# Decoder layer with linear attention on one core: a new order ahead of the first products and at the change of token halves, and output tiles in two banks

## The chip, the cores and the metric

One Trainium2 chip, one of its cores. The metric is device time in microseconds of one launch of the whole layer; the profile adds what each engine of the core did: TensorE (PE, with its weight loads as PEld), VectorE (DVE), ScalarE (ACT), GpSimd (POOL) and the queue of SyncE (SP), which issues transfers.

## What is computed

x is 2048 tokens (32 sequences of 64) by 512. Three steps, each with a residual:

```python
x = x + attn(layernorm(x))          # 32 heads of 128, decayed linear attention, gated
x = x + xattn(layernorm(x), ctx)    # cross attention, softmax over 512 positions
x = x + layernorm(x) @ identity.T
# attn: q, k, v = silu(h @ qkv_w.T); blocks of 32 tokens, scores decayed by head;
#       o * rsqrt(mean(o * o) + eps) * norm_w * sigmoid(h @ gate_w.T), then @ out_w.T
```

All in float32 precision. Only the first step is touched by the change.

## The kernel before

**Precision and products.** Each float32 operand is cut into a high part in a reduced format and a low part; a product is three matmuls (high by high, high by low, low by high). The projections use Strassen's scheme with seven block products in place of eight: the weights' blocks are mixed by four additions on GpSimd (mix, lines 302 to 309), the tokens' blocks by four subtractions (token_sums, lines 290 to 300). PRODUCTS (line 124) lists the seven with the bank that each adds to.

**Loops.** The tokens are two halves of 1024. For each half a body runs for d = 0 to 7 (quads of four heads): the first and the last body are written out, the six between are a hardware loop. A body is, on PE (lines 885 to 954): value products VA and VB (84 matmuls of 256 columns each), QK0, scores, QK1, scores, gate G01, weighing (two heads), QK2, output tiles 0 to 3 (rest_out), scores, QK3, output tiles 4 to 7, scores, G23, weighing. The second group's output tiles are made in the next body, in pairs behind VA, VB, QK0 and QK1. Each engine has its own list of the same body (GpSimd 337, ScalarE 505, VectorE 676), and only semaphores tie them. All orders are by hand.

**Within a call.** PE runs the seven products. The combinations go over snapshots: ScalarE copies a partial sum out of its bank (snapshot, line 431), VectorE adds it elsewhere (add_snapshot, 586), ScalarE takes the sigmoid, VectorE multiplies (silu, 593); GpSimd does the last block (321). ready_for (line 774) tells which product waits for which snapshot: the fifth for the second, the seventh for an addition on VectorE. Gaps in ScalarE's and VectorE's lists are filled with cuts of the next weights.

**Weights.** SP loads raw weights into raw0 and raw1; GpSimd mixes them; ScalarE writes the high part (cut_va and its like, 388 to 419), VectorE the low part (cut, 557); the second part's semaphore lets SP issue the next load (232 to 262). w_out goes the same way without mixing.

**Turning.** Tokens must lie with features on partitions. For a pair p of 128-token tiles (p and p + 4 of the half): statistics (652) and the root on GpSimd (283), normalise (661) writes the normed rows into qk or v (staged, 163), token_sums adds four blocks, PE transposes in four pieces of 4, 4, 4 and 2 blocks (turn, 845), ScalarE copies the high part (turned_hi, 495) and VectorE subtracts for the low part (turned_lo, 669). A pair's piece waits until the pair before has left the same bank.

**Start (lines 368 to 375, 541 to 548, 748 to 762, 956 to 959).** The weights of VA and VB are issued by SP behind the first two tiles. GpSimd: root and sums of pair 0, then both mixes, then the rest. Three pairs are turned ahead of VA, the fourth between VA and VB.

**Change of halves (lines 718 to 740, 943 to 950).** In the last body of the first half VectorE takes all eight statistics after QK3, normalises pair 0 after G23 and the others after the weighing. PE turns pair 0, makes output tiles 0 and 1, turns the other three and then begins the second half, with tiles 2 and 3 behind VA.

**Output banks (out_bank, 183).** Tiles 0 to 3 of the first group lie in banks 0, 1, 7, 0. Bank 7 is also that of the scores, so line 930 waits for the third addition ahead of them. The second group uses 0, 1, 0, 1. VectorE adds each tile into attn_acc (add_out, 643).

## Time and profile before

| | us |
|---|---|
| median of 3 runs | 2196.38 (2195.99 to 2198.97) |
| the profiled execution | 2197.48 |
| its span, first to last instruction | 2195.6 |
| PE busy | 2114.8 |
| DVE, ACT, POOL busy | 1450.6, 1136.8, 758.1 |

The mean granted clock of PE was 0.988 of full speed. A matmul counts as busy until its modelled end, and matmuls overlap, so PE's busy time is not PE at its peak. A row of the timeline gives start, length, engine, line, operation, output and inputs with their shapes, how many were merged, and in brackets the idle time ahead of it and what ended it. A wait counts only where the waiting engine is the one that everything else waits for.

### The profile page before, as it was taken

The page shows a single profiled execution, that of the slowest core. Times are in us where ns is not written, and L with a number is a line of the kernel's source. Part 1 is how long each engine was busy: PE and PEld are TensorE (multiplying, and loading weights), DVE is VectorE, ACT ScalarE, POOL GpSimd, SP SyncE. Part 2 cuts the span into 40 slices and gives each one's busy share as a digit, 9 for nine tenths or more (in the row PEclk, how much of TensorE's full clock was granted, in tenths as well). Part 3 has the DMA queues.
Part 4 walks back from the last instruction along what each step waited for, and adds up shares of the span by engine and source line. Part 5 has one row for each costly group of instructions (what it writes and reads, how often), then busy time and mean ns, then how long its engine had stood idle before and what let it go on. Part 6 is the DMA issues. An engine that isn't in the chain of part 4 may idle for free. (4 is left out here: it accounts for less than half of the span.)

```text
span 2195.6 us, 37208 instructions
## 1 busy us (share of the span) xinstructions
PE 2114.8 (96%) x13392; PEld 1752.8 (80%) x13392; DVE 1450.6 (66%) x2053; ACT 1136.8 (52%) x1927; POOL 758.1 (35%) x883
## 2 busy tenths in 40 slices
PE   4999999999999999989999999999999999699998
PEld 4788888888888888878888888888888888466665
DVE  5566657666666666766666666667666665588885
ACT  3554545454545555545454554545454554466664
POOL 6342425252434343343334342425252432111110
PEclk9999999999999999989999999999999999899999
DMA  2211111111212021111111111111111111301110
GB/s 89 79 50 50 49 49 49 49 49 38 60 32 66 29 65 34 46 35 40 60 40 56 42 49 49 49 49 49 47 51 38 60 31 50 127 30 44 49 44 20
DMA packets 40495, 109.37 MB, mean 50 GB/s; under 512 B 4960, under 2 KB 9568, under 8 KB 40288
## 3 DMA queue, kind: packets, MB, share of 16 engines
q1 hardware_dynamic: 40416, 108.30, 15.8%
q8 instruction: 51, 0.84, 0.2%
q14 instruction: 28, 0.23, 0.0%
HBM read 104.09 MB, written 4.19 MB: 49 GB/s over the span
## 5 line engine op out<-in xcount | busy, mean ns | idle before, releaser
L304 POOL TENSOR_TENSOR raw<-raw 128x256 f32<-128x256 f32 x128 | 100.7, 787 | 605.8 <-DMA raw<-w_pairs 605.7
L790 PE MATMUL bank<-x_hi,w_hi_c 128*128 128x512 f32 x672 | 266.1, 396 | 6.9 <-ACT gate L434 3.9
L795 PE MATMUL bank<-x_hi,w_lo_c 128*128 128x512 f32 x672 | 262.7, 391 | 0.0
L793 PE MATMUL bank<-x_lo,w_hi_c 128*128 128x512 f32 x672 | 262.3, 390 | 0.0
L840 PE MATMUL bank<-wo_hi,y_hi 128*128 128x512 f32 x512 | 202.5, 396 | 2.7 <-DVE y_lo L635 2.7
L841 PE MATMUL bank<-wo_lo,y_hi 128*128 128x512 f32 x512 | 201.9, 394 | 0.0
L842 PE MATMUL bank<-wo_hi,y_lo 128*128 128x512 f32 x512 | 201.9, 394 | 0.0
L434 ACT ACTIVATE qk<-bank 128x512 f32<-128x512 f32 x192 | 115.1, 600 | 143.6 <-PE bank L795 143.0
L335 POOL TENSOR_TENSOR sq_acc<-sq_acc,sq 128x512 f32<-128x512 f32 x124 | 160.2, 1292 | 81.9 <-ACT sq L486 68.7
L597 DVE TENSOR_TENSOR qk<-bank,qk 128x512 f32<-128x512 f32 x192 | 127.3, 689 | 85.2 <-ACT qk L457 42.6
L790 PE MATMUL bank<-x_hi,w_hi_a 128*128 128x512 f32 x448 | 177.9, 397 | 0.0
L649 DVE TENSOR_TENSOR attn_acc<-attn_acc,bank 128x512 f32<-128x512 f32 x240 | 162.5, 683 | 19.5 <-PE bank L842 18.4
L795 PE MATMUL bank<-x_hi,w_lo_a 128*128 128x512 f32 x448 | 174.8, 390 | 0.0
L793 PE MATMUL bank<-x_lo,w_hi_a 128*128 128x512 f32 x448 | 174.6, 390 | 0.0
L324 POOL TENSOR_TENSOR qk<-qk,sq 128x512 f32<-128x512 f32 x64 | 82.7, 1292 | 219.7 <-ACT sq L455 219.7
L790 PEld LDWEIGHTS bank<-x_hi,w_hi_c 128*128 128x128 f32 x672 | 126.5, 188 | 34.9 <-ACT gate L434 4.4
L795 PEld LDWEIGHTS bank<-x_hi,w_lo_c 128*128 128x128 f32 x672 | 126.5, 188 | 26.9
L590 DVE TENSOR_TENSOR bank<-bank,qk 128x512 f32<-128x512 f32 x128 | 89.6, 700 | 87.8 <-PE bank L795 87.0
L793 PEld LDWEIGHTS bank<-x_lo,w_hi_c 128*128 128x128 f32 x672 | 126.7, 188 | 25.1
L630 DVE TENSOR_TENSOR bank<-bank,gate 128x512 f32<-128x512 f32 x128 | 88.7, 697 | 79.9 <-ACT sq L486 78.1
L808 PE MATMUL bank<-w_hi_a,x_hi 128*128 128x256 f32 x448 | 130.1, 290 | 7.2 <-DVE x_lo L673 4.2
L590 DVE TENSOR_TENSOR gate<-bank,gate 128x512 f32<-128x512 f32 x96 | 66.4, 692 | 105.5 <-PE bank L795 105.5
(150 smaller groups left out, 5593.9 us busy)
## 6 DMA issues: line engine op xcount, KB each, us to landing
raw<-w_pairs SPq DMA_DIRECT2D x128, 512.0 KB, 3.5
raw<-w_out SPq DMA_DIRECT2D x32, 512.0 KB, 3.5
raw<-ctx_in SPq DMA_DIRECT2D x16, 256.0 KB, 2.9
raw<-ctx_in SPq DMA_DIRECT2D x32, 128.0 KB, 3.1
xr<-x SPq DMA_DIRECT2D x4, 1024.0 KB, 10.8
out<-attn_acc SPq DMA_DIRECT2D x16, 256.0 KB, 2.0
attn_acc<-x SPq DMA_DIRECT2D x8, 256.0 KB, 6.4
decays<-decay SPq DMA_DIRECT2D x32, 64.0 KB, 3.0
```

Of the source, the lines that this page charges most:

```text
L335: nc.gpsimd.tensor_tensor(acc, acc, sq[:, h], ALU.add).then_inc(sq_added, 1)
L434: nc.scalar.activation(dst, shaped(call, bank[:, (CHAIN, CHAIN, THIRD)[nth]]), ACT.Copy).then_inc(snapped, 1)
L590: nc.vector.tensor_tensor(dst, shaped(call, bank[:, (SECOND, CHAIN, THIRD)[nth]]), src, ALU.add).then_inc(c_added, 1)
L597: nc.vector.tensor_tensor(o, shaped(call, bank[:, at_bank]), o, ALU.mult).then_inc(silu_ready, 1)
L649: nc.vector.tensor_tensor(acc, acc, bank[:, out_bank(half, d, s, i)], ALU.add)\
L790: nc.tensor.matmul(bank[:, to], w_hi[w][:, a, s], x_hi[:, b, c], start=part in ("first", "only") and c == 0, stop=False, skip_group_check= ...
L793: nc.tensor.matmul(bank[:, to], w_hi[w][:, a, s], x_lo[:, b, c], start=False, stop=False, skip_group_check=True)
L795: i = nc.tensor.matmul(bank[:, to], w_lo[w][:, a, s], x_hi[:, b, c], start=False, stop=part in ("last", "only") and c == 1, skip_group_che ...
L808: nc.tensor.matmul(dst, x_hi[:, b, c, s], w_hi[c][:, a], start=part in ("first", "only") and c == 0 and j == 0, stop=False, skip_group_che ...
L840: nc.tensor.matmul(dst, y_hi[:, h, r], wo_hi[:, h], start=(h == 0), stop=False)
L841: nc.tensor.matmul(dst, y_hi[:, h, r], wo_lo[:, h], start=False, stop=False)
L842: k = nc.tensor.matmul(dst, y_lo[:, h, r], wo_hi[:, h], start=False, stop=(h == HG - 1))
```

## The change

Four things.

**Start.** The loads of VA's and VB's weights are issued by ScalarE at its very beginning, not by SP behind the first tiles. ScalarE then takes a sigmoid of a column that nobody reads. GpSimd mixes VA's weights before the first root and VB's before the second, then makes all token sums. Only pairs 0 and 1 are turned ahead of VA.

**Turning between value products.** In the first body of either half, the pieces of pairs 2 and 3 are turned ahead of the third, fifth and seventh product of VA (three, three and two pieces), with their copies on ScalarE and subtractions on VectorE in the gaps of VA; the cuts of QK0's weights move behind VA. In the second half these pieces use banks 0, 1 and 7.

**Last body of the first half.** The statistics are spread in pairs over four places, the root and the token sums are laid between GpSimd's other work, and each pair is normalised ahead of the first weighing, in QK2, before G23 and after it. Normed rows are written in place into attn_acc; the sums go to sq_acc, a new tensor, and the two halves of qk. Output tile 1 comes behind pair 1, tile 2 behind VA and tile 3 behind VB.

**Output tiles.** Both groups use banks 0 and 1 in turn for tiles 0 to 5; tile i waits for the addition of tile i - 2, and the wait ahead of the scores is gone.

The diff, cut to its core, with eight columns of indentation taken off:

```diff
...
+sigmoid_set = sb(own, "sigmoid_set", [P, 1])
+spare_sums = sb(own, "spare_sums", [P, 2 * BT])
...
-def staged(p, cols):
-    row = cols.start // 512
-    if p % 2 == 0:
-        return qk[:, row // 2, row % 2, cols.start - 512 * row:cols.stop - 512 * row]
-    return v[:, row // 2, 2 + row % 2, cols.start - 512 * row:cols.stop - 512 * row]
+def normed(half, p):
+    return [attn_acc[:, half * HT + p + TT * row, c * 2 * P:(c + 1) * 2 * P] for row in range(2) for c in range(2)]
+def summed(p):
+    home = (sq_acc[:, 2 * BT:], spare_sums[:, :], qk[:, 0].rearrange("p k n -> p (k n)"),
+            qk[:, 1].rearrange("p k n -> p (k n)"))[p]
...
+def piece(half, p, r):
...
+    return ((b11, b21), (b22, t1), (t2, t3), (t4n,))[r]
+def whole(*tiles):
+    return tuple((p, r) for p in tiles for r in range(4))
+WITH_VALUES = whole(2)[:3], whole(2)[3:] + whole(3)[:2], whole(3)[2:]
...
-def turn_bank(half, r):
...
+def turn_bank(half, p, r):
+    if half == 1 and p >= 2:
+        return (0, 1, 7)[(4 * (p - 2) + r) % 3]
...
-def out_bank(half, d, s, i):
-    if s == 0:
-        return (0, 1, 7, 0, 0, 1, 5, 6)[i]
+def out_bank(i):
...
-            if p == 0:
-                load(raw1, w_pairs[0, VA], raw1_landed)
-                load(raw0, w_pairs[0, VB], raw0_landed)
...
+            if half == 1 and p >= 2:
+                pool.wait_ge(s_mm, count(0, LAST, 4, 4))
...
                 mix0(half, d, 1)
-            mix1(half, d, 1, 2)
-            last_block(half, d, VA)
+                last_block(half, d, VA)
+                mix1(half, d, 1, 2)
+            else:
+                mix1(half, d, 1, 2)
+                last_block(half, d, VA)
...
             last_block(half, d, QK0)
             mix0(half, d, 3)
             last_block(half, d, QK1)
+            if half == 0 and at(d, LAST):
+                inv_roots(slice(0, HT), 2 * HT, TT + 1)
             mix1(half, d, 2, 4)
             squares(half, d, 0)
             mix0(half, d, 4)
             last_block(half, d, QK2)
+            if half == 0 and at(d, LAST):
+                token_sums(1, 0)
...
                 mix1(half, d, 3, 5)
                 mix0(half, d, 5)
+            if half == 0 and at(d, LAST):
+                token_sums(1, 1)
             last_block(half, d, QK3)
+            if half == 0 and at(d, LAST):
+                token_sums(1, 2)
...
-                inv_roots(slice(0, HT), 2 * HT, TT + 1)
-                token_sums(1, 0)
+                token_sums(1, 3)
             squares(half, d, 1)
-            if half == 0 and at(d, LAST):
-                for p in range(1, TT):
-                    token_sums(1, p)
-        for p in range(TT):
-            inv_roots(slice(p, HT, TT), 2 * p + 2, p + 1)
-            if p:
-                token_sums(0, p - 1)
-            if p == 1:
-                mix1(0, 0, 0, 1)
-                mix0(0, 0, 0)
-        token_sums(0, TT - 1)
+        mix1(0, 0, 0, 1)
+        inv_roots(slice(0, HT, TT), 2, 1)
+        mix0(0, 0, 0)
+        inv_roots(slice(1, HT, TT), 4, 2)
+        token_sums(0, 0)
+        token_sums(0, 1)
+        inv_roots(slice(2, HT, TT), 6, 3)
+        token_sums(0, 2)
+        inv_roots(slice(3, HT, TT), 8, 4)
+        token_sums(0, 3)
...
-            project(half, d, VA, lambda: cut_qk0(half, d, 0), lambda: cut_qk0(half, d, 1))
-            if first:
-                turned_hi(0, 3)
+            if at(d, 0):
+                project(half, d, VA, *(lambda i=i: turned_hi(half, WITH_VALUES[i]) for i in range(3)))
+                for part in range(2):
+                    cut_qk0(half, d, part)
+            else:
+                project(half, d, VA, lambda: cut_qk0(half, d, 0), lambda: cut_qk0(half, d, 1))
...
-                for p in range(TT):
-                    turned_hi(1, p)
+                turned_hi(1, whole(0, 1))
...
-        turned_hi(0, 0)
+        for raw, call, landed in ((raw1, VA, raw1_landed), (raw0, VB, raw0_landed)):
+            act.dma_start(raw[:, 0:4], w_pairs[0, call].rearrange("p (r n) -> p r n", r=4)).then_inc(landed, 16)
+        act.wait_ge(consts_set, 2)
+        nc.scalar.activation(sigmoid_set[:, :], ones[:, 0:1], ACT.Sigmoid)
...
-        turned_hi(0, 1)
...
+        turned_hi(0, whole(0, 1))
...
-        turned_hi(0, 2)
...
-            if p >= 2:
-                dve.wait_ge(x_turned, (half * TT + p - 1) * 4)
-            for r, t in enumerate((p, p + TT)):
-                nc.vector.tensor_scalar(staged(p, slice(r * 512, (r + 1) * 512)), attn_acc[:, half * HT + t],
+            for t in (p, p + TT):
+                nc.vector.tensor_scalar(attn_acc[:, half * HT + t], attn_acc[:, half * HT + t],
...
-            project(half, d, VA, lambda: cut_c(half, d, 0, 0))
-            cut_c(half, d, 0, 1)
+            before_turning = half == 0 and at(d, LAST)
+            if at(d, 0):
+                project(half, d, VA, lambda: turned_lo(half, WITH_VALUES[0] + WITH_VALUES[1]),
+                        lambda: turned_lo(half, WITH_VALUES[2]))
+                for part in range(2):
+                    cut_c(half, d, 0, part)
+            else:
+                project(half, d, VA, lambda: cut_c(half, d, 0, 0))
+                cut_c(half, d, 0, 1)
...
-                for i in ((2, 3) if turning else (0, 1)):
+                for i in ((2,) if turning else (0, 1)):
...
-            else:
-                turned_lo(0, 3)
+            if before_turning:
+                dve.wait_ge(x_rest_landed, 16)
+                statistics(1, (0, TT), HT)
...
-                for i in (() if turning else (2, 3)):
+                for i in ((3,) if turning else (2, 3)):
...
+            if before_turning:
+                statistics(1, (1, TT + 1), HT + 2)
...
+            if before_turning:
+                statistics(1, (2, TT + 2), HT + 4)
...
+            if before_turning:
+                statistics(1, (3, TT + 3), HT + 6)
             decay_scores(half, d, 0, 1)
...
+            if before_turning:
+                normalise(1, 0)
             weighted(half, d, 0)
             project(half, d, QK2, lambda: cut_a(half, d, 2, 0))
+            if before_turning:
+                normalise(1, 1)
...
-            if half == 0 and at(d, LAST):
-                dve.wait_ge(x_rest_landed, 16)
-                statistics(1, range(HT), HT)
...
             decay_scores(half, d, 1, 1)
+            if before_turning:
+                normalise(1, 2)
...
-            if half == 0 and at(d, LAST):
-                normalise(1, 0)
+            if before_turning:
+                normalise(1, 3)
...
-            if half == 0 and at(d, LAST):
-                dve.wait_ge(pv_mm, count(half, d, 8, 8))
-                normalise(1, 1)
-                turned_lo(1, 0)
+            if before_turning:
+                turned_lo(1, whole(0))
...
+                turned_lo(1, whole(1))
...
-                normalise(1, 2)
-                turned_lo(1, 1)
-                normalise(1, 3)
-                turned_lo(1, 2)
-                turned_lo(1, 3)
...
-        statistics(0, (2, 2 + TT), 4)
-        normalise(0, 1)
-        turned_lo(0, 0)
-        statistics(0, (3, 3 + TT), 6)
...
-        normalise(0, 2)
-        turned_lo(0, 1)
+        normalise(0, 1)
+        statistics(0, (2, 2 + TT), 4)
...
+        turned_lo(0, whole(0, 1))
+        normalise(0, 2)
+        statistics(0, (3, 3 + TT), 6)
...
-        turned_lo(0, 2)
...
             for n, (a, b, to, part) in enumerate(PRODUCTS):
+                if call == VA and at(d, 0) and n in (2, 4, 6):
+                    turn(half, WITH_VALUES[n // 2 - 1])
...
-        def turn(half, p):
-            n = half * TT + p
...
+        def turn(half, pieces):
...
+                n = half * TT + p
                 if r == 0:
...
-                if p:
-                    pe.wait_ge(x_ready, 4 * (n - 1) + r + 1)
-                first = PIECES[r].start
-                for c in range((PIECES[r].stop - first) // P):
-                    k = nc.tensor.transpose(bank[:, turn_bank(half, r), c * P:(c + 1) * P],
-                                            staged(p, slice(first + c * P, first + (c + 1) * P)), ident[:, :])
+                order = 4 * (p - 2) + r
+                if half == 1 and p >= 2 and order >= 3:
+                    pe.wait_ge(x_ready, 4 * n + r - 2)
+                elif half == 1 and p >= 2 and order < 2:
+                    pe.wait_ge(out_added, count(0, LAST, 16, 9 + order))
+                elif p:
+                    pe.wait_ge(x_ready, 4 * n - 3 + (r if half == 0 or p < 2 else 3))
+                for j, block in enumerate(piece(half, p, r)):
+                    for c in range(2):
...
+                        k = nc.tensor.transpose(bank[:, turn_bank(half, p, r), to:to + P],
+                                                block[:, c * P:(c + 1) * P], ident[:, :])
...
-                if i == 2 and s == 1:
-                    pe.wait_ge(out_added, count(half, d, 16, 9))
-                if i == 3:
-                    pe.wait_ge(out_added, count(half, d, 16, 8 * s + (1, 2)[s]))
...
-                    pe.wait_ge(out_added, count(half, d, 16, 8 * s + (4, 3)[s]))
-                if i == TT + 1:
-                    pe.wait_ge(out_added, count(half, d, 16, 8 * s + 4))
+                if 2 <= i < 6:
+                    pe.wait_ge(out_added, count(half, d, 16, 8 * s + i - 1))
...
             if at(d, 0):
-                pe.wait_ge(x_ready, 16 * half + 8 if half == 0 else 32)
+                pe.wait_ge(x_ready, 16 * half + 8)
             else:
...
+            if at(d, 0):
+                pe.wait_ge(x_ready, 16 * half + 16)
...
-                rest_out(*previous, 1, (2, 3) if turning else (0, 1))
-            else:
-                turn(0, 3)
-                pe.wait_ge(x_ready, 16)
+                rest_out(*previous, 1, (2,) if turning else (0, 1))
...
-            if previous and not turning:
-                rest_out(*previous, 1, (2, 3))
+            if previous:
+                rest_out(*previous, 1, (3,) if turning else (2, 3))
...
-            pe.wait_ge(out_added, count(half, d, 16, 3))
...
-                turn(1, 0)
-                rest_out(half, d, 1, (0, 1))
-                turn(1, 1)
-                turn(1, 2)
-                turn(1, 3)
+                turn(1, whole(0))
+                rest_out(half, d, 1, (0,))
+                turn(1, whole(1))
+                rest_out(half, d, 1, (1,))
...
-        turn(0, 0)
-        turn(0, 1)
-        turn(0, 2)
+        turn(0, whole(0, 1))
...
```

## Rows read from the trace of the kernel before

**Rows 1.** the page's first part, busy us of each engine, share of the span, instructions

```profile
PE 2114.8 (96%) x13392; PEld 1752.8 (80%) x13392; DVE 1450.6 (66%) x2053; ACT 1136.8 (52%) x1927; POOL 758.1 (35%) x883
```

**Rows 2.** stretches: us, then PE, PEld, DVE, ACT, POOL busy, clock, DMA, GB/s

```profile
32.80:54.10 21.30, 15.45 (x100) 15.01 (x98) 10.79 (x17) 9.24 (x16) 11.50 (x14) 0.84 0.20 61
...
943.70:965.80 22.10, 16.62 (x101) 13.09 (x100) 18.41 (x31) 12.27 (x24) 18.90 (x24) 0.86 0.01 2
965.80:992.30 26.50, 24.96 (x180) 24.24 (x181) 11.73 (x18) 10.97 (x18) 4.73 (x6) 0.92 0.07 20
1078.90:1191.70 112.80, 112.09 (x709) 96.14 (x708) 72.59 (x103) 57.89 (x93) 43.02 (x46) 1.00 0.16 49
1915.50:2185.00 269.50, 263.67 (x1839) 169.89 (x1838) 218.01 (x317) 171.56 (x391) 31.48 (x90) 1.00 0.12 39
```

**Rows 3.** timeline of the start: start us, us, instruction, [idle before <- releaser]

```profile
9.14 1.38 DVE L656 BATCH_NORM_STATS2 stats<-attn_acc 128x6 f32<-128x512 f32 x2 [3.39 <-DMA attn_acc<-x]
...
19.33 2.84 DVE L559 TENSOR_TENSOR w_lo_a<-raw,w_hi_a 128x1024 fp32r<-128x1024 f32 x2 [0.59 <-ACT w_hi_a L386]
...
24.49 1.11 PE L856 MATMUL bank<-ident,v 128*128 128x128 f32 x4 [7.56 <-POOL v L295]
...
32.83 0.56 PE L808 MATMUL bank<-w_hi_a,x_hi 128*128 128x256 f32 x1
...
40.21 1.28 ACT L442 ACT_TABLE_LOAD   x1
...
54.12 0.39 PE L808 MATMUL bank<-w_hi_a,x_hi 128*128 128x256 f32 x1 [2.88 <-DVE x_lo L673]
...
67.44 0.47 PE L790 MATMUL bank<-x_hi,w_hi_c 128*128 128x512 f32 x1 [1.50 <-DVE v L597]
```

**Rows 4.** timeline of the last body of the first half

```profile
871.14 0.70 DVE L590 TENSOR_TENSOR bank<-bank,qk 128x512 f32<-128x512 f32 x1
...
872.50 0.60 ACT L434 ACTIVATE qk<-bank 128x512 f32<-128x512 f32 x1
...
873.67 0.39 PE L790 MATMUL bank<-x_hi,w_hi_a 128*128 128x512 f32 x1
...
922.93 4.83 DVE L656 BATCH_NORM_STATS2 stats<-attn_acc 128x6 f32<-128x512 f32 x8
...
934.99 1.33 ACT L427 ACTIVATE wo_hi<-raw,normw 128x512 fp32r<-128x512 f32 x2 [4.44 <-DMA raw<-w_out]
...
937.92 0.50 PE L790 MATMUL bank<-x_hi,w_hi_c 128*128 128x512 f32 x1 [3.93 <-ACT gate L434]
```

**Rows 5.** timeline of the change of halves and the first calls after it

```profile
943.75 3.73 PE L831 MATMUL bank<-scores,v 128*128 128x128 f32 x32
...
946.91 5.71 POOL L335 TENSOR_TENSOR sq_acc<-sq_acc,sq 128x512 f32<-128x512 f32 x4
...
950.20 1.85 ACT L498 ACTIVATE x_hi<-bank 128x512 fp32r<-128x512 f32 x4
...
953.64 1.23 PE L856 MATMUL bank<-ident,v 128*128 128x128 f32 x8 [1.60 <-DVE x_lo L673]
...
965.86 0.58 PE L808 MATMUL bank<-w_hi_a,x_hi 128*128 128x256 f32 x1 [1.32 <-DVE x_lo L673]
...
992.33 0.47 PE L790 MATMUL bank<-x_hi,w_hi_c 128*128 128x512 f32 x1 [1.50 <-DVE v L597]
```

**Rows 6.** timeline of a looped body, from the first output tile to the scores

```profile
227.58 0.40 PE L840 MATMUL bank<-wo_hi,y_hi 128*128 128x512 f32 x1
...
229.94 0.68 DVE L649 TENSOR_TENSOR attn_acc<-attn_acc,bank 128x512 f32<-128x512 f32 x1
...
231.67 0.68 DVE L649 TENSOR_TENSOR attn_acc<-attn_acc,bank 128x512 f32<-128x512 f32 x1
...
233.14 1.28 DVE L649 TENSOR_TENSOR attn_acc<-attn_acc,bank 128x512 f32<-128x512 f32 x2
...
234.04 1.15 PE L823 MATMUL bank<-qk 128*64 128x64 f32 x32 [0.71 <-DVE attn_acc L649]
```

41 lines of the change are left out of this document (24 added, 17 removed).

## The prediction

> **What bounds the kernel now.** I read the busy shares first: TensorE has a matmul in flight for 2114.8 of the 2195.6 us [rows 1]. So the time moves only where TensorE stands still or runs at the lower of its two clock levels. The second view is the table by stretches: one whole looped body has PE busy in 112.1 of 112.8 us at a granted clock of 1.00, while the first 21 us of value products have 0.84, and the 22.1 us in which the second token half is turned have 16.6 us busy at 0.86 [rows 2]. What is to be won lies at these two places. The timeline of the start shows which wait ends last there: PE sits 7.56 us ahead of the second tile pair, behind GpSimd, which mixes weights between two pairs; the first value product comes at 32.8 us; ScalarE loads a table at 40.2; the second value call starts at 54.12 and QK0 at 67.44 [rows 3]. Ahead of the half change eight statistics in one piece (4.83 us) push VectorE's cuts, so w_out is requested late, ScalarE waits 4.44 us for it, and the snapshot behind it holds PE for 3.93 us [rows 4]. Then come turns with waits of 1.60 us and less between them [rows 5]. Last, a wait of 0.71 us before the scores in each looped body [rows 6].
>
> **Start.** The weights' two loads go to ScalarE's queue, GpSimd mixes them first, and only two tile pairs are turned ahead of the first value products; the other two go between the products. The bytes are the same, and no more of them stand ahead of the second pair, so its statistics begin by 9.14 as now [rows 3] or a little sooner; normalising starts near 10.2. Then VectorE's queue decides: normalise 1.0, cut A 2.2 (2.84 with GpSimd beside it [rows 3]), normalise 1.0 to 1.8, two statistics 1.4, cut B 2.2 to 2.8, first low part 0.6. GpSimd's second root is ready at 13.0 to 14.7 (landing about 5, mix 2.9, root 1.1, mix 2.9 to 4.6, root 1.1). From the first low part on, the second pair's 14 transposes take 3.9 us at the half clock (4 take 1.11 [rows 3]) and the last piece's copy, subtraction and hops 1.4. The sum is 24.0 at best and 26.7 at worst; I take 25.3 for the first value product against 32.83.
>
> The VA call then lasts: 84 products at 0.12 us are 10.1; 17 of them at the half clock (before, it rose with the ninth product or so) add 1.6; 28 transposes at 0.12 add 3.4; waits on the parts 0.2; after the last product a sigmoid, the last low parts and the product on VectorE take 2.0, where no other PE work stands. That is 17.3. VB and its tail take 10.1 + 1.65. QK0 starts at 25.3 + 29.05 = 54.35. The 2 us wait may bring one stretch at the half clock, as the wait of 2.88 us at 54.12 probably did [rows 3]; one of 6.8 us would cost 3.0, I book 1.0 and keep 0 and 3.0. Against 67.44 that is **-12.1**, with ends -14.4 and -8.1. The table load leaves the chain: its 1.28 us [rows 3] now runs while nothing has landed. What covers the rest: QK0's weights are mixed on GpSimd by 37 and cut behind VA by 43.5, ten microseconds ahead of need. SP is not moved past a new wait; its next loads hang on cut B, which ends at 18 to 20 instead of 32.
>
> **Last body of the first half.** The same statistics are spread over four places, each 1.45 us, and four normalisations of 1.0 us come in. VectorE's slack ahead of the next snapshot addition is 2.2 us after VA (costs nothing), 0.7 before QK0 and 0.6 before the gate (cost 0.1 and 0.25). At QK1 there is none: the addition starts at 871.14 right behind the decays, the snapshot that the fifth product waits for starts at 872.50 and ends 0.6 later, and that product starts at 873.67 [rows 4]. So of 1.45 us delay 0.85 reaches PE. The second normalisation stands ahead of the output additions, which PE waits for there (below): 1.05. The others fall in slack. Sum +2.2; removed is the 3.93 us wait and the half clock of 3.4 us behind it (1.7). The gate call starts at 930.4 and hands over at 940.2, against 943.75: -3.5.
>
> **Turning.** Now 22.1 us lie between the first weighing and the value products [rows 2]. GpSimd reaches the squares 3.2 us after the weighing begins [rows 5]; in the new order the last token sums stand ahead of them and it gets there after 3.45. ScalarE, which has to square in between, begins copying turned parts at 6.85 us instead of 6.45 (950.20 against 943.75 [rows 5]). VectorE subtracts the first tile in 2.2 us, adds one output tile in 0.6, subtracts the second in 2.2: ready 12.6 us after the weighing, so value products start at 952.8 against 965.86: -13.0, of which 3.5 are those above. Within VA, 28 transposes (3.4) and the tail (2.0, of which output tile 2 covers nothing, since the call waits for all parts first; the tile then covers the wait for VB) give 16.65 us to the start of VB, and 28.4 to QK0, against 26.47 in the rows [rows 5], where tiles 2 and 3 and the half clock are inside. That gives back 1.95. The clock: now 0.92 in that stretch [rows 2]. In the new order PE idles 1.6 us before and 1.1 us after the last turns; I book 1.5 for one half-clock stretch reaching into VA and keep 0 and 3.0. Sum **-9.6**; with 1.5 more for VectorE and GpSimd getting in each other's way the ends are -11.1 and -6.5.
>
> What the clock does when transposes stand between products is shown in the last stage of the kernel: hundreds of them between matmuls, and the granted clock is 1.00 over 269.5 us [rows 2]. The Trainium skill (TensorE: Matmul & The Clock Gate, Part 4: PE-mode transpose) says the opposite, that transpose mode does not count as PE activity for the gate. By the row the sum is the one below; by the rule both VA calls could run at the half clock, and the sum would be that of rival (b), 2195.
>
> **Two banks.** In each of 16 bodies output tile 2 no longer takes bank 7. Now the scores wait for the third addition. In the loop tile 0's first matmul starts at 227.58; the additions end at 3.04, 4.77 and 6.24 us after it, and the scores start at 6.46 [rows 6]. New: tile 2 waits for the first addition until 3.09 (it could start at 2.79), tile 3 for the second until 4.82, lasts 1.39 plus 0.11 for a matmul after a wait, and the scores start at 6.42. The wait moves and stays as long: VectorE's queue sets it. The four unrolled bodies should differ from this by a tenth of a microsecond at most (an estimate by the same working). Total **0**; ends -1.6 (no restart cost) and +2.9 (each wait 0.17 dearer).
>
> **The sum.** -12.1 - 9.6 + 0 = -21.7. The profiled execution took 2197.48 us (its span 2195.6 and 1.9 around it), 1.1 above the median of 2196.38. So 2197.48 - 21.7 - 1.1 = **2174.7**. The ends add to -27.1 and -11.7: 2169.3 to 2184.7.
>
> **Rivals.** (a) The start gives nothing: the value products begin sooner, but a later supplier (mixing for QK0 or QK1, GpSimd's queue) puts QK0 where it is. For it speaks that GpSimd was the releaser there [rows 3]; against it ten microseconds of lead. 2174.7 + 12.1 = 2186.8. Chance 0.10.
>
> (b) PE runs both turning VA calls at the half clock. 84 products lose 0.093 us each and 28 transposes 0.16: 12.3 per call, less what is booked, near 10; with both, 2195, no change. Against it stands the last stage at 1.00 [rows 2]; for it, that the clock fell in the stretch where PE did transposes with waits between [rows 2, 5]. Chance 0.06. It is what the Trainium skill's rule above would make of this change.
>
> (c) Slower: the place is tiles 2 and 3 in all 16 bodies. Two short waits in place of one let the clock fall for one stretch of 3.4 us in each body, 1.7 us of loss, 27 in all: 2174.7 + 27 = 2201.7. It decides once a body loses over 1.63 us. Against it: a wait of 0.71 us leaves the clock of the looped body at 1.00 [rows 2, 6]. Chance 0.04.
>
> The forecast itself has 0.80, with 2169 to 2185 as its own range. The whole range adds (a) and a part of (b): 2167 to 2187. A measurement of this kernel tells apart about 0.2%, 4.4 us. Faster by more: forecast and (a), 0.90; within: 0.06; slower: 0.04.
>
> **What would show it.** First value product near 25 us and QK0 near 55; no table load at 40; no 3.9 us wait near 934; the value products of half two 12.6 us after the last weighing begins, near 941; the scores' wait gone and two waits of 0.3 us in its place on output matmuls. A first VA call over 20 us long, or a first product later than 28, would prove the start wrong; a granted clock under 0.8 in VA is (b); under 1.00 in looped bodies is (c).

## The result, and the profile after

The changed kernel takes **2177.14 us** (median of 4 runs, 2175.81 to 2177.40) against 2196.38: the ratio is 0.9908, with a 95% interval of 0.9896 to 0.992. So 19.2 us are gone, with 21.7 forecast: the time lies 2.4 us above the forecast and inside the range. Its profiled execution took 2177.07 us with a span of 2175.0. One execution of a kernel further down (`add_first`) took 3490.83 us at a mean granted clock of 0.558; the times compared there are those of its other four.

The page's first part of the changed kernel answers to [rows 1]. TensorE's busy time fell by only 1.6 us, so nearly all of the gain is idle time that went.

```profile
PE 2113.2 (97%) x13392; PEld 1742.6 (80%) x13392; DVE 1454.7 (67%) x2053; ACT 1134.4 (52%) x1927; POOL 758.1 (35%) x883
```

The stretches answer to [rows 2]: the first call of value products (VA), the way from the last weighing of the first half to the value products of the second, VA there, and a looped body.

```profile
26.30:43.50 17.20, 15.50 (x112) 15.30 (x112) 11.67 (x23) 8.71 (x17) 13.01 (x19) 1.00 0.01 1
...
929.50:942.60 13.10, 10.41 (x73) 8.61 (x72) 10.03 (x18) 8.04 (x16) 11.68 (x14) 1.00 0.01 1
942.60:959.10 16.50, 15.22 (x118) 14.38 (x119) 10.01 (x17) 9.59 (x17) 1.29 (x1) 1.00 0.01 1
...
1096.00:1208.80 112.80, 112.60 (x709) 96.26 (x708) 73.62 (x103) 58.08 (x92) 43.14 (x46) 1.00 0.16 48
```

Both VA calls hold 28 transposes between their products. The turning stretch shrank from 22.1 to 13.1 us. The clock column has 1.00 for both calls, where the first had 0.84 before; but for the first call it can't be taken at its word. In the profile before and in this one it reads 1.00 from the start of the span on, and the rows beneath it say otherwise: here the first 22 products start 0.21 us apart, and from 31.2 us on they start 0.12 us apart, which are the paces of the lower and of the upper level (in half two of the kernel before, products 0.21 us apart go with a granted clock of 0.50). Before the change it was the first eight.

```profile
30.79 0.41 PE L854 MATMUL bank<-w_hi_a,x_lo 128*128 128x256 f32 x1
...
33.97 0.28 PE L852 MATMUL bank<-w_lo_b,x_hi 128*128 128x256 f32 x1
```

In the second VA call the products are 0.12 us apart from the first on, so there the 1.00 holds.

The timeline of the start answers to [rows 3]. GpSimd has its first weights at 4.94, the sigmoid's table is loaded at 1.65, while nothing has landed, and the first value product comes at 26.35 instead of 32.83. The two rows of 11.25 and 11.88 stand side by side: while VectorE cuts (it reads two tiles in SBUF), a mix on GpSimd takes 1.70 instead of 0.72 us.

```profile
1.65 1.28 ACT L572 ACT_TABLE_LOAD   x1 [1.65 <-PEq L1478]
...
4.94 0.72 POOL L320 TENSOR_TENSOR raw<-raw 128x256 f32<-128x256 f32 x1 [4.07 <-DMA raw<-w_pairs]
...
11.25 3.14 DVE L589 TENSOR_TENSOR w_lo_a<-raw,w_hi_a 128x1024 fp32r<-128x1024 f32 x2
...
11.88 1.70 POOL L325 TENSOR_TENSOR raw<-raw 128x256 f32<-128x256 f32 x1
...
26.35 0.58 PE L849 MATMUL bank<-w_hi_a,x_hi 128*128 128x256 f32 x1 [1.32 <-DVE x_lo L703]
```

The Trainium skill (GPSIMD Engine Reference, 1. Specifications) says that GpSimd shares its ports into SBUF with VectorE, and that VectorE's instructions with two inputs there contend with it. The pair of rows agrees, with 1.70 against 0.72 us.

Next the timeline of the last body of the first half and of the turning, which answers to [rows 4, 5].

```profile
862.10 0.50 PE L829 MATMUL bank<-x_hi,w_hi_a 128*128 128x512 f32 x1 [0.50 <-ACT qk L459]
...
895.24 1.42 DVE L696 TENSOR_SCALAR attn_acc<-attn_acc,mv,rstd 128x512 f32<-128x512 f32 x2
896.58 1.47 DVE L589 TENSOR_TENSOR w_lo_a<-raw,w_hi_a 128x768 fp32r<-128x768 f32 x1
897.98 0.68 DVE L681 TENSOR_TENSOR attn_acc<-attn_acc,bank 128x512 f32<-128x512 f32 x1
898.71 0.50 PE L881 MATMUL bank<-wo_hi,y_hi 128*128 128x512 f32 x1 [1.95 <-DVE attn_acc L681]
...
930.66 0.60 ACT L513 ACTIVATE sq<-bank 128x512 f32<-128x512 f32 x1 [0.29 <-PE bank L872]
933.28 0.60 ACT L513 ACTIVATE sq<-bank 128x512 f32<-128x512 f32 x1 [2.02 <-PE bank L872]
...
936.96 1.85 ACT L525 ACTIVATE x_hi<-bank 128x512 fp32r<-128x512 f32 x4
```

The wait of 3.93 us is gone. In its place stand small ones: 0.50 at QK1, and 1.95 us ahead of the third output tile, for an addition that stands behind a normalisation (1.42 us) and a cut (1.47 us). Before, the same cut took 0.95 us; now GpSimd adds token sums up to 897.24, into its time.

```profile
905.95 0.95 DVE L559 TENSOR_TENSOR w_lo_a<-raw,w_hi_a 128x768 fp32r<-128x768 f32 x1
```

Last a looped body, which answers to [rows 6].

```profile
217.90 0.68 DVE L681 TENSOR_TENSOR attn_acc<-attn_acc,bank 128x512 f32<-128x512 f32 x1
218.63 0.19 PEld L881 LDWEIGHTS bank<-wo_hi,y_hi 128*128 128x128 f32 x1 [0.57 <-DVE attn_acc L681]
...
219.63 0.68 DVE L681 TENSOR_TENSOR attn_acc<-attn_acc,bank 128x512 f32<-128x512 f32 x1
...
220.36 0.19 PEld L881 LDWEIGHTS bank<-wo_hi,y_hi 128*128 128x128 f32 x1 [0.51 <-DVE attn_acc L681]
...
221.96 1.15 PE L864 MATMUL bank<-qk 128*64 128x64 f32 x32
```

The one wait of 0.71 us ahead of the scores became two ahead of the weight loads of output tiles 2 and 3, and their first matmuls come 0.30 and 0.23 us later than the pace of 0.23 us would have them. From the first output matmul to the scores it is 6.42 us (215.54 to 221.96) where it was 6.46.

Starts of the same instructions in both profiles give the ledger. Each row is the lead of the changed kernel over the kernel before at that place:

| place | before | after | lead |
|---|---|---|---|
| first value product | 32.83 | 26.35 | 6.5 |
| QK0 of the first body | 67.44 | 55.35 | 12.1 |
| QK0 of the last body, half one | 854.59 | 842.29 | 12.3 |
| gate | 881.72 | 870.31 | 11.4 |
| QK3 | 911.83 | 903.11 | 8.7 |
| last weighing, half one | 943.75 | 929.57 | 14.2 |
| value products of half two | 965.86 | 942.69 | 23.2 |
| QK0 of half two | 992.33 | 970.84 | 21.5 |
| last output tiles of attention | 1879.61 | 1857.32 | 22.3 |
| end of the span | 2195.6 | 2175.0 | 20.6 |

The lead is won at the two places that the forecast named, held through the loops, and 1.7 us of it are lost again from the last output tiles on, where the change adds no work. 1.6 us are lost in these tiles themselves: their 24 matmuls take 7.00 us (1857.32 to 1864.32), where they took 5.44, and the first of them start 0.43 us apart instead of 0.23. These two stretches of the changed kernel show the clock there; columns as in [rows 2].

```profile
1855.00:1875.00 20.00, 14.48 (x66) 10.05 (x68) 7.74 (x12) 3.86 (x6) 3.02 (x2) 0.73 0.31 112
1875.00:1895.00 20.00, 9.29 (x44) 5.17 (x36) 11.30 (x18) 10.69 (x25) 2.52 (x6) 0.59 0.58 203
```

The same two of the kernel before, 22 us later:

```profile
1877.00:1897.00 20.00, 14.62 (x77) 9.33 (x75) 8.76 (x12) 5.89 (x12) 3.02 (x2) 0.83 0.38 141
1897.00:1917.00 20.00, 9.45 (x48) 6.23 (x48) 12.41 (x20) 10.53 (x22) 2.53 (x6) 0.66 0.53 192
```

The work is the same, and the granted clock is 0.73 and 0.59 instead of 0.83 and 0.66. At the lower level (half of the upper) that is 20 x (0.27 + 0.41) x 2 = 27 us against 20 x (0.17 + 0.34) x 2 = 20. Seven microseconds more at half speed, in a passage where TensorE is busy for some 0.6 of the time, agree with the loss of 1.7.

### The profile page after: what moved, and what is told of

Read it like the earlier page. It is cut to its first block and busy times, and to the rows that moved or that the text cites. A ratio compares the mean times of both kernels' runs of the same rounds, so it can differ in the third digit from the quotient of the medians.

```text
span 2175.0 us, 37218 instructions
## 1 busy us (share of the span) xinstructions
PE 2113.2 (97%) x13392; PEld 1742.6 (80%) x13392; DVE 1454.7 (67%) x2053; ACT 1134.4 (52%) x1927; POOL 758.1 (35%) x883
## 3 DMA queue, kind: packets, MB, share of 16 engines
q10 hardware_dynamic: 288, 1.05, 0.1%
```

## The experiments

Two theories were tried. Mine: the gain is that of fewer and later turns ahead of the products, plus rows that are normalised and summed ahead of the change of halves; the two banks give nothing, since VectorE's order sets that wait. The rivals: that the banks carry a part, that the spread statistics alone carry the half change, or that the interleaving does. Ratios are to the kernel before, measured on the same chip as each kernel; its median there was 2196.38 to 2197.32 us. Differences to the changed kernel under 2 us are read from the profiles, since the medians alone hardly tell them apart.

**The old banks in the changed kernel.**

```diff
-            return (0, 1, 0, 1, 0, 1, 5, 6)[i]
+            return ((0, 1, 7, 0, 0, 1, 5, 6), (0, 1, 0, 1, 0, 1, 5, 6))[s][i]
```

Its waits go back to their old places with it.

> The changed kernel with the old banks (0, 1, 7, 0 for tiles 0 to 3 of the first group, and the wait for the third addition ahead of the scores). My theory: VectorE's queue of additions sets when the scores start, whichever tile waits for it. So the scores of a looped body start again 6.4 to 6.5 us after the first output matmul, and each body is within 0.15 us of the changed kernel's; over all 16 bodies 0 to +1.5 us. Rival: the two banks carry a part of the gain worth naming, 0.3 us a body or more, so +5 us.

One execution took 2175.03 us, 2.1 under the median of the changed kernel, with the loops as long as in the changed kernel: from QK0 of the first body to QK0 of the last in half one they are 0.17 us apart, and from QK0 of the first body to the last weighing of half two by nothing. The view of the addition's line says who waits for it now:

```profile
who waited for it (us, times):
  PE bank L864: 10.6, 14
```

The scores (L864) again wait 0.71 us in the timeline of each looped body. So the banks move the wait and don't shorten it. What differs in the end is the clock: 1870 to 1900 has 0.72 here and 0.64 in the changed kernel, and the last output tiles take 5.5 us here and 7.0 there.

**The spread statistics alone, in the kernel before.**

```diff
+                    spread = half == 0 and at(d, LAST)
+                    if spread:
+                        dve.wait_ge(x_rest_landed, 16)
+                        statistics(1, (0, TT), HT)
                     project(half, d, VB)
...
-                        statistics(1, range(HT), HT)
```

The other three pairs stand behind VB, the cuts of QK0 and QK1, as in the change.

> The kernel before with one part of the change alone: the eight statistics of the second half stand in pairs at four places of the last body. My theory: the block of 4.83 us delayed the cuts, these w_out, and this the snapshot that held PE for 3.93 us and let the clock fall behind it (1.6 us). Both go; the statistics ahead of QK1's and the gate's additions cost 0.8 and 0.3. So -4.4 us, 2192.0. Rival: moving the statistics only moves the time, VectorE is late in four places instead of one: 0 to -1 us.

2192.14 us against 2197.32 (ratio 0.9977, interval 0.9967 to 0.9987): 5.2 us, where 4.4 were expected. In the profile the last body gives 4.6 of it between its QK0 and the last weighing. The delays that the new places cost are those of the changed kernel (0.8 us at QK1, 0.3 at the gate), so the price is the statistics', not the normalisations'. From the last weighing to QK0 of half two it is 47.5 us, where it was 48.6: without the other parts the half change stays about as long. The microsecond is the clock's, which was at the lower level before the value products (0.77) and not in them (1.00, before 0.92 [rows 2]):

```profile
943.90:965.90 22.00, 16.39 (x93) 14.33 (x92) 16.20 (x28) 11.22 (x22) 15.46 (x19) 0.77 0.00 1
961.20:987.70 26.50, 24.96 (x188) 23.97 (x189) 12.80 (x18) 11.20 (x19) 6.30 (x8) 1.00 0.06 20
```

**All pairs of the second half turned ahead of its value products.** In the changed kernel; copies and low parts of all four pairs go ahead of the call.

```diff
-                        if call == VA and at(d, 0) and n in (2, 4, 6):
+                        if call == VA and half == 0 and at(d, 0) and n in (2, 4, 6):
...
-                        turned_hi(1, whole(0, 1))
+                        turned_hi(1, whole(0, 1, 2, 3))
```

> The changed kernel, in the second half all four pairs are turned ahead of the first value product, nothing between the products; all else stays. My theory: the turning is set by the copies and subtractions (2.2 us a pair on VectorE) and costs nearly the same in either place. The value products start 5 to 6 us later and the call is 4.9 us shorter, so +0.3 to +1.5 us, and 1.5 to 3 more if the clock falls in the longer stretch of transposes: +1 to +4. Rival: overlapping the turns with products is what saved the 9 us between weighing and products, so +6 us or more.

2178.35 us (ratio to before 0.9918, interval 0.9902 to 0.9935): 1.2 above the changed kernel's 2177.14, inside the 1 to 4 expected. The intervals of the two ratios overlap, so the profile has to decide. Counted from the last weighing, the products start 6.4 us later, but VB only 1.7 and QK0 1.8 later. From the last weighing to QK0 the change shortened the way from 48.6 to 41.3 us, and 1.8 of these 7.3 us are the interleaving's. By subtraction the greater part is left to the rows that are normalised and summed ahead, and some of it to the clock (0.86 and 0.92 before [rows 2]); no run takes either away alone. The windows also answer the question of the clock: all turning, with waits between the turns, and the products behind it are at 1.00.

```profile
933.00:949.70 16.70, 11.42 (x78) 8.93 (x76) 13.13 (x23) 10.66 (x21) 9.23 (x10) 1.00 0.01 2
949.70:960.80 11.10, 11.02 (x88) 10.89 (x89) 3.51 (x7) 4.26 (x8) 1.30 (x1) 1.00 0.00 0
```

**All pairs of the first half ahead.** The same edit for the first half.

```diff
-                        if call == VA and at(d, 0) and n in (2, 4, 6):
+                        if call == VA and half == 1 and at(d, 0) and n in (2, 4, 6):
...
-                turn(0, whole(0, 1))
+                turn(0, whole(0, 1, 2, 3))
```

> The changed kernel, in the first half all four pairs are turned ahead of the first value product. My theory: here GpSimd's sums of pairs 2 and 3 are what the products would have to wait for; they end at 35.3 us, so the first product starts near 36.7 instead of 26.35, the call is 5 us shorter, and QK0 comes 5 us later: +5 us, 2182. Rival: the gain of the start comes from GpSimd's order and from both mixes standing first, so leaving the turns ahead costs 1 us or less.

2182.74 us (0.9935, 0.9918 to 0.9952): 5.6 above the changed kernel, 5 expected; in the profile QK0 is 7.1 us later. Here interleaving pays, since the products stand against waits for late suppliers instead of behind them. The timeline has the first product at 37.23, and the window around it shows the lower clock level, which ends inside its call:

```profile
37.23 0.58 PE L856 MATMUL bank<-w_hi_a,x_hi 128*128 128x256 f32 x1 [1.32 <-DVE x_lo L706]
```

```profile
34.00:42.00 8.00, 6.41 (x33) 5.82 (x33) 2.50 (x6) 2.21 (x5) 3.83 (x6) 0.57 0.00 0
```

**Without the sigmoid of an unused column.** The table is then loaded when VA needs it.

```diff
-                nc.scalar.activation(sigmoid_set[:, :], ones[:, 0:1], ACT.Sigmoid)
```

> The changed kernel without the sigmoid of the unused column, so that the table is loaded at the first sigmoid of VA. My theory: the load of 1.28 us delays VectorE's multiplication and behind it the low parts of pair 2, for which the transposes of pair 3 wait; the fifth product starts 1.2 us later: +1.2 us. Rival: ScalarE and VectorE have slack there and the load is hidden: 0.

2178.56 us (0.9915, 0.9899 to 0.9932), 1.4 above the changed kernel, but the ranges of the runs touch (2176.79 to 2180.32 against 2175.81 to 2177.40). The profile is clearer than the time: the load stands in the middle of VA, and VB starts at 44.85 instead of 43.54.

```profile
33.62 1.28 ACT L467 ACT_TABLE_LOAD   x1
34.92 0.60 ACT L467 ACTIVATE v<-bank 128x512 f32<-128x512 f32 x1
```

The Trainium skill (ScalarE: Activation LUTs, What ACT_TABLE_LOAD costs) gives 1283 ns for the load, which the row shows, and 1380 ns more for a drain. The second is not seen: the activation behind the load starts 1.38 us later (34.92) than in the changed kernel (33.54).

**The first weights on SyncE's queue again,** behind the first tile pair.

```diff
+                    if p == 0:
+                        load(raw1, w_pairs[0, VA], raw1_landed)
+                        load(raw0, w_pairs[0, VB], raw0_landed)
```

> The changed kernel with the first two weight loads issued by SP behind the first two tiles, as before the change. My theory: the first weights land at 6.4 us instead of 4.9 and the second pair of tiles 0.8 us later; both of the chains that lead to the second normalisation get 1 us later, so the first product starts at 27.3 instead of 26.35: +1.0 us. Rival: on the shared DMA engines the order makes no difference to what the chain waits for: 0.

2177.18 us (0.9909, 0.9892 to 0.9925), the same as the changed kernel. Its profile does not agree with "no effect": the weights land at 8.51 instead of 4.94, the second pair's statistics wait for their rows until 10.37, and the first product is 3.0 us later.

```profile
8.51 0.72 POOL L323 TENSOR_TENSOR raw<-raw 128x256 f32<-128x256 f32 x1 [7.64 <-DMA raw<-w_pairs]
...
10.37 1.37 DVE L689 BATCH_NORM_STATS2 stats<-attn_acc 128x6 f32<-128x512 f32 x2 [4.61 <-DMA attn_acc<-x]
```

```profile
29.38 0.58 PE L850 MATMUL bank<-w_hi_a,x_hi 128*128 128x256 f32 x1 [1.32 <-DVE x_lo L704]
```

QK0 is 2.4 us later, and the span of this execution 1.3 longer. Its four runs scatter by more than that (2175.0 to 2178.4), so the worth of the second queue stays between 0 and 2.4 us. My expected 1.0 is neither shown nor refuted.

**The normalisation that stood ahead of the additions, moved** into QK3's call, where VectorE waits for TensorE.

```diff
-                    if before_turning:
-                        normalise(1, 1)
                     cut_a(half, d, 2, 1)
...
-                    project(half, d, QK3)
+                    project(half, d, QK3, (lambda: normalise(1, 1)) if before_turning else None)
```

> The changed kernel with the normalisation of pair 1 moved from QK2's end into the 2.0 us in which VectorE waits inside QK3. My theory: the 1.95 us wait of PE ahead of output tile 2 in this body falls back to that of a normal body (0.25 and 0.35 in two places): -1.3 us. Rival: the wait has another cause (the contended cut ahead of the addition) and stays: 0.

2174.70 us (0.9899, 0.9882 to 0.9916): 2.4 under the changed kernel, 1.3 expected; in the profile 1.9 from QK0 to QK3 of the last body. The cut behind takes 0.98 us again, and the wait of 1.95 us has shrunk to what every looped body has:

```profile
896.12 0.19 PEld L879 LDWEIGHTS bank<-wo_hi,y_hi 128*128 128x128 f32 x1 [0.55 <-DVE attn_acc L681]
...
897.86 0.19 PEld L879 LDWEIGHTS bank<-wo_hi,y_hi 128*128 128x128 f32 x1 [0.51 <-DVE attn_acc L681]
```

**The statistics as well,** into VB, ahead of QK0 and into QK1.

```diff
-                    project(half, d, VB)
+                    project(half, d, VB, (lambda: statistics(1, (1, TT + 1), HT + 2)) if before_turning else None)
...
-                    project(half, d, QK1)
+                    project(half, d, QK1, (lambda: statistics(1, (3, TT + 3), HT + 6)) if before_turning else None)
```

> The one before, and three of the four pairs of statistics stand where VectorE waits for PE inside a call or has slack: inside VB, behind it ahead of QK0, and inside QK1. My theory: the 0.5 us wait in QK1 and the loss at the gate go too: -2.4 us in all, 2174.7. Rival: the sum of VectorE's work sets the time and moving it inside the calls delays the additions there as much: -1.3 us.

2172.70 us (0.9889, 0.9873 to 0.9906): 2.0 under the one before it and 1.5 in the profile, 1.1 expected as the difference of the delays at QK1 and the gate. No wait is left at QK1. From QK0 to the weighing the last body lasts 83.9 us (841.58 to 925.44), against 87.3 in the changed kernel and 89.2 before, of which the wait of 3.93 and the clock behind it (1.7) make 5.6. That leaves 0.3 us, so nearly all added work is hidden now.

**The changed kernel once more,** with no edit, for its scatter and its clock.

> The changed kernel itself once more, beside the others of this call. My theory of the end: where the clock's steps fall at the passage to the cross attention differs from run to run and moves a profile by up to 2 us, so its time is 2177 with single runs from 2175 to 2179. Rival: each kernel has its own fixed place for them, then all its runs agree within 0.5 us.

2176.68 us (0.9907, 0.9891 to 0.9924). The profile has the same work, but its clock fell elsewhere: 1870 to 1900 has 0.69 where the first profile of the same kernel has 0.64.

```profile
1870.00:1900.00 30.00, 19.20 (x104) 11.17 (x105) 19.04 (x27) 15.90 (x36) 2.52 (x6) 0.69 0.60 211
```

Here a stretch of 3.4 us at the lower level begins at 898.6, just behind the wait for the third output tile, where the first profile has none. VA of the first half differs as well: its products are 0.12 us apart from 26.5 on, where the first profile has 22 of them at 0.21. Yet QK0 comes only 0.5 us sooner (54.83), since TensorE waits 1.09 us for the low parts of pair 2, ahead of the fifth product.

```profile
26.87 0.28 PE L854 MATMUL bank<-w_hi_a,x_lo 128*128 128x256 f32 x1
...
35.15 1.01 PE L903 MATMUL bank<-ident,attn_acc 128*128 128x128 f32 x6 [1.09 <-DVE x_lo L703]
```

So these stretches are no fixed property of a kernel, and a profile says their cost to about 2 us.

**Each addition of an output tile one place earlier.** Of VectorE's work behind QK2 the first addition goes ahead of the cut, and so on: addition, cut, addition, cut, addition, cut, addition.

```diff
+                    add_out(half, d, 0, 0)
                     cut_a(half, d, 2, 1)
                     for i in range(2):
-                        add_out(half, d, 0, i)
+                        add_out(half, d, 0, 1 + i)
                         cut_c(half, d, 2, i)
-                    add_out(half, d, 0, 2)
                     add_out(half, d, 0, 3)
```

> The changed kernel, in QK2's tail of every body each output addition stands one place earlier in VectorE's list: addition 0, cut A, addition 1, cut C, addition 2, cut C, addition 3. My theory: what holds PE in the looped body, with old banks or new, is that the additions queue behind the cuts. Now the first ends 2.3 us after the first output matmul and the second at 3.8, before tiles 2 and 3 could start (2.8 and 4.2), so the wait of 0.65 us goes in all 16 bodies: -10.5 us, 2166.5. Rival: the cuts get later, and with them the loads and mixes of the next weights, so the wait comes back in QK3 or the gate: -2 us or less.

2163.05 us (ratio 0.985, 0.9833 to 0.9866) against 2176.68 for the changed kernel on the same chip: **13.6 us, more than any other single edit here gives,** with 10.5 expected. The waits are read from the last kernel below, which has the same order.

**The token sums behind the squares,** so that GpSimd reaches them earlier.

```diff
+                    squares(half, d, 1)
                     if half == 0 and at(d, LAST):
                         token_sums(1, 3)
-                    squares(half, d, 1)
```

> The changed kernel, the token sums of pair 3 of the second half behind GpSimd's squares instead of ahead of them. My theory: the squares gate ScalarE's second pair of squares and with them the start of its copies of turned parts; GpSimd gets to them 2.5 us sooner, the sums are needed only in the middle of VA: the value products of the second half start 2 us earlier, -2 us. Rival: what holds ScalarE there is not GpSimd but a wait of 2.0 us of its own ahead of the second square, with no engine late in the profile, beside an instruction fetch: it stays, and the gain is 1 us or less.

2175.09 us (0.9899, 0.9883 to 0.9916) against 2176.68: not told apart, since the ranges overlap. From the last weighing to the products it is 12.4 instead of 13.1 us. GpSimd comes to the squares 1.8 us after the weighing begins instead of 4.1, but ScalarE does not go on:

```profile
932.16 1.27 POOL L351 TENSOR_TENSOR sq_acc<-sq_acc,sq 128x512 f32<-128x512 f32 x1 [0.88 <-ACT sq L513]
...
934.02 0.60 ACT L513 ACTIVATE sq<-bank 128x512 f32<-128x512 f32 x1 [1.94 <-POOL sq_acc L351]
```

The view of the DMA queues for the changed kernel, 931 to 933, has one packet in its gap between the same two squares:

```profile
q14 instruction: 1, 0.01, 1.8%
```

It is a fetch of instructions. Two kernels above vary this place without touching it. With both weight loads back on SyncE's queue ScalarE's list is shorter ahead of it, and the second square follows the first after 0.30 us, as in the kernel before. Without the sigmoid and its table load the gap is 0.96 us. In the nine other profiles of the changed kernel and its variants it is 1.8 to 2.0. So the gap goes with what stands ahead in ScalarE's list and not with a releaser, which fits the fetch; but no run keeps the code and takes the fetch away. These rows are of the kernel with the loads on SyncE's queue, where the weighing begins at 932.07:

```profile
934.06 0.60 ACT L516 ACTIVATE sq<-bank 128x512 f32<-128x512 f32 x1 [0.30 <-PE bank L873]
...
936.18 4.12 POOL L354 TENSOR_TENSOR sq_acc<-sq_acc,sq 128x512 f32<-128x512 f32 x3
```

GpSimd begins its squares 4.1 us behind the weighing there, as in the changed kernel, and ScalarE's copies of turned parts start as late (7.4 us). So two limits of the same size stand side by side, and taking away either alone gives little.

**All together:** the additions first, the normalisation and statistics in gaps, the sums behind the squares, and three small edits: at the start the third pair's statistics go ahead of the second pair's normalising; at the half change the turned pieces take their banks in another order, so that a late addition is waited for later; and output tile 2 goes ahead of the wait for VA's last pieces.

```diff
-                return (0, 1, 7)[(4 * (p - 2) + r) % 3]
+                return (7, 1, 0)[(4 * (p - 2) + r) % 3]
...
-                normalise(0, 1)
                 statistics(0, (2, 2 + TT), 4)
+                normalise(0, 1)
...
-                    if at(d, 0):
-                        pe.wait_ge(x_ready, 16 * half + 16)
+                    if turning:
+                        pe.wait_ge(x_ready, 30)
                     if previous:
                         rest_out(*previous, 1, (2,) if turning else (0, 1))
+                    if at(d, 0):
+                        pe.wait_ge(x_ready, 16 * half + 16)
```

> Everything that paid, in one kernel: the additions one place earlier in QK2's tail, pair 1 normalised inside QK3, the statistics of the last body in VectorE's gaps, the token sums of pair 3 behind the squares; and two untried ones: the statistics of pair 2 of the first half ahead of the second normalisation, in a wait of VectorE's, and output tile 2 at the change of halves ahead of the last turned parts (the pieces of pairs 2 and 3 take banks 7, 1, 0 so that its bank is free). My theory: the gains lie at different places and add: from 2163.05 (additions) 2 for the statistics and the normalisation, 1.0 for the first products, 0.7 for the squares, 0.9 for tile 2: 2158.5 us. Looped bodies have no wait of PE over 0.2 us. Rival: the gains compete for the same slack of VectorE, and 2161 to 2163 is all.

**2157.69 us** (2156.95 to 2158.83; ratio 0.9822, interval 0.9808 to 0.9835), with 2158.5 expected: 0.9% under the changed kernel and 1.8% under the one before. The three small edits were not run alone. In a window of looped bodies TensorE has a matmul in flight all the time:

```profile
1050.00:1163.80 113.80, 113.80 (x725) 98.26 (x724) 75.03 (x104) 58.96 (x95) 44.81 (x48) 1.00 0.15 48
```

Its timeline of a looped body shows the scores' weights loaded with no wait for an addition, and an addition running beside the scores:

```profile
235.48 1.01 PEld L858 LDWEIGHTS bank<-qk 128*64 128x64 f32 x32 [0.37 <-issue]
...
235.93 0.68 DVE L681 TENSOR_TENSOR attn_acc<-attn_acc,bank 128x512 f32<-128x512 f32 x1
```

The first output matmul starts at 229.81 and the scores at 235.49: 5.68 us against 6.42. That is 0.74 per body and 11.8 in sixteen. The groups of the two pages, first the changed kernel's, say it as a sum over all of them:

```profile
L881 PE MATMUL bank<-wo_hi,y_hi 128*128 128x512 f32 x512 | 206.7, 404 | 9.2 <-DVE y_lo L667 3.3
```

```profile
L875 PE MATMUL bank<-wo_hi,y_hi 128*128 128x512 f32 x512 | 203.5, 397 | 3.1 <-DVE y_lo L667 3.1
```

Beside the idle time (9.2 to 3.1 us), 3.2 us of busy time went (a matmul after a wait takes 0.50 instead of 0.39 us); the rest stands ahead of the weight loads. Of the 13.6 us the order explains 11.8; what the others are, clock or the last body, stays open, and 1.8 us is within what two runs of one kernel differ by.

## Why the prediction was right, and where not

- **The start, -12.1 forecast, -12.1 measured at QK0.** Errors cancelled, so the exact hit is luck. The first product came at 26.35, 1 us behind the 25.3 taken and inside 24.0 to 26.7: the mix beside the cut (1.70 us) put GpSimd's second root at 15.3, where 14.7 was the latest forecast. The 1.0 booked for a fall of the clock at VB wasn't needed (VB's products are 0.12 us apart). VA, 17.3 forecast, took 17.2, but 22 products ran at the lower pace and not 17, and the transposes took less than their 3.4. `as_changed` shows that a late supplier stood close behind: with no product at the lower pace, VA is only 0.7 us shorter. Rival (a), a late supplier that puts QK0 where it was, fell. The kernel with all first pairs ahead (`first_ahead`) shows that 5.6 us hang on the interleaving. What the new order on GpSimd gives by itself was not run. The upper end of the start's range does not come out of its terms: 26.7 + 29.05 + 3.0 is 58.75, so -8.7 and not -8.1, and 2184.1 for the whole.
- **The last body of half one, -3.5 forecast, 1.9 measured.** The delays at QK1 (0.85 forecast, 0.8 measured) and the gate (0.25, 0.3) were right. Mis-sized is the step "The second normalisation stands ahead of the output additions ...: 1.05": QK3 lost 2.4 us more. From VectorE's last multiplications for QK2 (894.00) to the first addition (897.98) it is 3.98 us, where it was 2.11: the pair's normalisation took 1.42 us and not 1.0, the cut behind it 1.47 instead of 0.95, and all of it reached PE, since VectorE was the later one there already. `norm_in_gap` takes the term away: 1.9 us in the profile, 2.4 in the medians. Of the 0.5 us that its QK2 to QK3 is still longer than before (17.47 against 16.95), 0.4 go when the statistics are moved as well (17.10 in `stats_in_gaps`).
- **The turning, from the weighing on: 12.6 us forecast, 13.1 measured.** -9.5 forecast, -9.0 measured. Mis-sized is "it gets there after 3.45": GpSimd began the squares 4.12 us after the weighing, since its last token sums, which stand ahead, could start only 1.25 us after it, when VectorE had normalised their rows. ScalarE's own gap of 2.0 us ahead of its second square, which the sum didn't have, is a second limit of the same size: `sums_behind_squares` takes the first away and gains 0.7 us in the profile, `weights_on_sp` lacks the second and gains nothing there.
- **VA of half two, 28.4 us forecast to QK0, 28.15 measured.** The call's 16.65 does not come out of the terms named (10.1, 3.4 and 2.0 make 15.5), yet 16.4 was measured, because output tile 2 (1.5 us) stands behind the wait for all parts. The 1.5 booked for the clock was not needed in this profile; `no_preset` and `weights_on_sp` have a stretch of 3.4 us at the lower level between the last weighing and the products, and their way to QK0 is 0.6 and 0.4 us longer. Together with the body the half change is -9.2 against -9.6: a loss that I hadn't seen (1.35 at the normalisation, 0.5 at the squares) against one that I had booked and that did not come (1.5). That too is luck in part.
- **Rival (b)** would have had both VA calls at the lower level. The second ran at 1.00, and so did in `second_ahead` the stretch in which all four pairs are turned. The first began at the lower pace and left it after 22 of its 84 products, with the transposes still to come. The rule of the Trainium skill (TensorE: Matmul & The Clock Gate, Part 4: PE-mode transpose) by which transposes don't count as activity is not borne out in any run of this case: in `as_changed` TensorE had done nothing but transposes when its first product came, and the products behind it start 0.12 us apart, the pace of the upper level.
- **Two banks, 0 forecast, -0.3 measured** over the loops of both halves. The working was right: the two tiles come 0.30 and 0.23 us late, 0.3 each forecast, and the tail is 6.42 long, the very figure of the sum. Rival (c), a clock that falls in each body for them, fell: looped bodies are at 1.00.
- **The end of the span,** where I had put no step: 1.7 us of the lead went to a lower granted clock, 1.6 of them in the last output tiles. Between the two profiled executions the difference is 20.4 us (2197.48 to 2177.07), 1.3 short of the sum of 21.7; without those 1.7 it would have been met. The other 1.1 of the 2.4 us are the median's: the profiled execution before lay 1.1 above its median, which the sum took off, and that of after lies on its own.

## What to carry to other kernels

When one short wait stands in every body, read what the late engine does ahead of the releasing instruction: here a change of buffers moved a wait of 0.71 us, and an exchange in VectorE's order took it away: 13.6 us, beside 19 for the whole of the large change. Work that is added to an in-order queue costs nothing only inside a gap in which this engine waits for the bottleneck; the same statistics and the second normalisation make the last body 3.4 us longer at their convenient places than inside such gaps. A booking for the clock is a range, not a term: profiles of the same kernel had their slow stretches at different places, with 1.6 us at stake in the last output tiles alone. And where the clock column and the distance of equal matmuls disagree, as in the first 31 us here, go by the distance.

## What the hardware showed that I had not expected

- The granted clock of the same kernel falls at different places from one execution to the next (0.64 and 0.69 in the same 30 us), in a passage where DMA is busy for 0.6 of the time and TensorE for about 0.6.
- The wait of 1.95 us ahead of the third output tile was followed by 3.4 us at the lower level in four profiles (`second_ahead`, `no_preset`, `as_changed`, `sums_behind_squares`) and by none in three others that have it (the changed kernel's own, `first_ahead` and `weights_on_sp`).
- Behind much the same transposes the first value products ran at the lower pace (0.21 us apart) for 14 to 22 products in six profiles of the changed kernel and its variants, and at the upper (0.12) from the first in five. The clock column had 1.00 ahead of the first product in all of them but `first_ahead`.
- ScalarE stood for 1.8 to 2.0 us between two squares, with a fetch of instructions in the gap of the changed kernel, and for 0.3 us where two loads fewer stood in its list ahead of that place. That it waits for the fetch is argued, not shown.
